# Sixteen graphs through four graph layers on one core: half weighings first in the filling, and one attention's row of powers made by way of DRAM

## The chip, the cores and the metric

The kernel runs on one core of one Trainium2 chip. The metric is the device time of one execution in microseconds (us), the median of several runs; less is better.

## The reference, cut to what matters

There are 16 graphs of N = 1024 nodes with 128 features and a 0/1 adjacency. Four layers follow one another, each `x = x + layer(relu(layernorm(x)), adj)`. The first is a convolution with batch norms over all graphs. Layers 1 and 3 are additive attentions, layer 2 a product attention:

```
e = leaky_relu(s[:, None] + t[None, :], 0.2)         # s, t = Wh @ a_src, Wh @ a_dst
attn = softmax(where(adj > 0, e, -big)); out = attn @ Wh      # layer 3: elu(out)
```

The kernel calls layer 1 A, layer 2 B and layer 3 C. Since exp of a leaky relu of a sum is the larger of two products, A and C need, after factors are taken out, only `weights = max(row, least[j]) * mask`: `row` holds 1024 powers exp(0.8 us) of the scores, the same on all 128 partitions (`row_e`), and `least` one value for each of the 8 partition tiles j. `us` (128 x 8) has the same scores, one to a partition and tile.

## The kernel before, in words

The first layer takes two stages (up to about 440 us of the profile); the third, on which the change bears, holds the other three. Its rounds i = -1 to 18 (`run(i)` on each engine) form a pipeline over graphs: round i weighs A of graph i, then B of graph i - 1, then C of graph i - 2. Rounds 0, 1 and 2 are the **filling**: round 0 has A alone, round 1 A and B, and from round 2 on all three run. There is no planner: for each engine the order is written out by hand in its `run(i)` (DVE L1084, ACT L1401, PE L1650) and in the loops of SP (L823) and POOL (L864), and semaphores join the queues.

- **PE.** `weigh(x, b, c)` (L1584) makes output tile c of 8: eight matmuls over j into a slot of PSUM, two tiles to a slot; `take` waits until the slot's last user is through. The profile has two records for each fp32 matmul, so a tile is 16 records and a weighing of 8 tiles 128. `weigh_half` (L1602) makes tiles 0 to 3 with j outermost, so that each weights tile j serves four output tiles as soon as it is made; before, only the last C uses it. `gram` (L1562) makes B's scores. `turn_h` (L1528), `turn_q` (L1521) and `turn_rows` (L1574) transpose. `values` (L1550) makes Wh, `highest` (L1545) the top of the scores, and `rows` (L1535) spreads one half of `us` over a row by four transposes.
- **PE's order in a round:** `turn_h` of C, the eight `gram` steps with C's `values`, `highest` and first `rows` between them (L1661 to L1670), A's eight tiles with `turn_q`, C's second `rows` and `turn_rows` between them, B's eight tiles with the next A's `turn_h`, `values`, `highest` and `rows`, then C's eight tiles.
- **DVE.** `weights(x, b, j)` (L938) makes one tile of weights. `exponents` (L915) makes `us` and `te`. `shares` (L964) takes the reciprocals of the sums of a finished pair of tiles, `add` (L972) the residual, then come `stats`, `moments` and `shifts` of the next norm. `leaky` and `lower` work on B, `split_g` and `split_ag` make the low halves for `gram`.
- **ACT.** `row_power` (L1299) makes one half of `row_e` from PSUM, `exps` (L1290) makes `least`, `scaled` (L1327) divides a pair of tiles, which frees their slot, `factors` (L1307) makes A's weighed values, `keep_scores` and `score_exps` follow `gram`, `normed` applies a norm, `high_scores` feeds the splits.
- **POOL.** `upper` (L853) masks B's upper rows, eight steps, each after the turned rows of its k; A's `rstd` stands after the second of them.
- **SP.** Loads in a fixed order: A's mask ring (four tiles deep, in pairs), `qT`, C's ring, B's mask, x, and the output.

## Time and profile before

| | |
|---|---|
| median of 3 runs | 1531.18 us (1531.07 to 1531.24) |
| the profiled execution | 1534.19 us |
| its span in the profile | 1532.4 us |
| PE busy | 1402.3 us (92% of the span) |
| DVE busy | 1133.6 us (74%) |
| ACT busy | 826.6 us (54%) |
| POOL busy | 380.9 us (25%) |
| mean granted TensorE clock | 0.963 |

Busy time is summed over the instructions of an engine, and the share is that of the whole span, so an engine with a high share can still stand idle in one stage. A row of a timeline gives the start, the length, the engine, the line of the code, the operation with the tile that it writes and those that it reads, the number of merged instructions and, in brackets, how long the engine had been idle and who ended that. A matmul's end is modelled, so that a row of PE can end some 0.2 us after the next begins: lengths are better taken from start to start. "q" behind an engine marks its queue, that is the issue of a DMA.

### The profile page before, as it was taken

What the parts mean: (1) busy time and instruction counts of PE and PEld (TensorE: products, weight loads), DVE (VectorE), ACT (ScalarE), POOL (GpSimd) and SP (SyncE); (2) the same over time, 40 slices, a digit from 0 to 9 for tenths busy, and PEclk for the clock granted to TensorE, in tenths of its full rate; (3) what the DMA queues carried; (4) which work ended last, traced back from release to release, by engine and by line L of the source; (5) the groups of instructions that cost most, each with busy time, mean ns of one, the idle gap of its engine ahead of it and who ended that gap; (6) DMA issues with size and microseconds to landing.
All of it is one profiled execution on the core that took longest, in us unless ns stands there. A gap on an engine that the chain in (4) does not pass through costs nothing.

```text
span 1532.4 us, 33041 instructions
## 1 busy us (share of the span) xinstructions
PE 1402.3 (92%) x12740; PEld 1269.2 (83%) x12740; DVE 1133.6 (74%) x3270; ACT 826.6 (54%) x1825; POOL 380.9 (25%) x337
## 2 busy tenths in 40 slices
PE   5899999799946679999999999999999999999886
PEld 5899999555536469999999998989999999999786
DVE  4566665687834667888888888888888888887565
ACT  4687778022232455746656566556574665655521
POOL 6334340000010214133132231331313313232120
PEclk9899999799968789999999999999999999999998
DMA  9999992376741122231431313313223143131111
GB/s 206 225 199 206 211 212 69 103 252 233 247 152 45 52 77 76 56 90 38 109 90 50 97 47 93 104 36 104 72 74 90 36 110 90 36 83 22 49 42 43
DMA packets 109599, 161.95 MB, mean 106 GB/s; under 512 B 9472, under 2 KB 61312, under 8 KB 107392
## 3 DMA queue, kind: packets, MB, share of 16 engines
q1 hardware_dynamic: 85248, 117.86, 26.7%
q0 software_dynamic: 19584, 33.56, 11.9%
q10 hardware_dynamic: 4608, 8.39, 1.6%
q8 instruction: 102, 1.67, 0.4%
q14 instruction: 57, 0.47, 0.1%
HBM read 151.40 MB, written 41.94 MB: 126 GB/s over the span
## 4 chain that ended last, share of the span: by engine, by line
PE 44%; DVE 13%; ACT 6%; DVEq 3%; POOL 2%; issue 2%; DMA 0%; ACTq 0%
PE ps L1598 27%; PE ps L1557 4%; DVE wts_A L946 3%; PE ps L1580 3%; PE ps L1532 2%; PE ps L1569 2%; POOL rs_C L851 2%; DVE wts_C L946 2%; PE ps L1571 2%; PE ps L1570 2%; ACT hN L1279 1%; ACT hV L1276 1%; PE ps L1541 1%; DVEq L979 1%; DVE st_C L884 1%
## 5 line engine op out<-in xcount | busy, mean ns | idle before, releaser
L1598 PE MATMUL ps<-hP_A,wts_A 128*128 128x129 f32 x2112 | 255.3, 276 | 3.7 <-DVE wts_A L946 3.0
L862 POOL TENSOR_TENSOR wts_B<-wts_B,off 128x1024 f32<-128x1024 f32 (+7 forms) x128 | 174.5, 1388 | 335.8 <-PE ps L1580 335.8
L1598 PE MATMUL ps<-hV,wts_B 128*128 128x129 f32 x2048 | 246.5, 276 | 4.4 <-DVE wts_B L961 2.6
L1598 PEld LDWEIGHTS ps<-hP_A,wts_A 128*128 128x128 f32 x2112 | 245.3, 192 | 5.0 <-DVE wts_A L946 4.0
L1598 PEld LDWEIGHTS ps<-hV,wts_B 128*128 128x128 f32 x2048 | 238.8, 193 | 5.3 <-issue 3.0
L1598 PE MATMUL ps<-hP_C,wts_C 128*128 128x129 f32 x1920 | 220.1, 274 | 0.0
L1598 PEld LDWEIGHTS ps<-hP_C,wts_C 128*128 128x128 f32 x1920 | 217.4, 191 | 0.5
L946 DVE SCALAR_TENSOR_TENSOR wts_A<-row_A,least_A,ring_A 128x1024 f32<-128x1024 f32 x128 | 160.8, 1274 | 7.5 <-ACT row_A L1304 4.7
L294 ACT ACTIVATE maskT<-ps 128x1024 fp8e4<-128x1024 bf16 x128 | 131.2, 1025 | 59.5 <-PE ps L336 48.2
L946 DVE SCALAR_TENSOR_TENSOR wts_C<-row_C,least_C,ring_C 128x1024 f32<-128x1024 f32 x120 | 160.2, 1346 | 0.0
L348 PE MATMUL ps<-x,adj_b 128*128 128x129 f16 x896 | 122.4, 225 | 16.1 <-ACT whn L277 13.1
L1338 ACT ACTIVATE xB<-ps,rec_A 128x128 f32<-128x128 f32 x128 | 40.1, 364 | 165.1 <-DVE rec_A L970 165.1
L349 PE MATMUL ps<-x,adj_b 128*128 128x128 f16 x896 | 122.7, 224 | 0.0
L952 DVE SCALAR_TENSOR_TENSOR wts_B<-wts_B 128x1024 f32<-128x1024 f32 (+7 forms) x128 | 90.7, 750 | 34.5 <-ACT wts_B L1320 34.5
L348 PEld LDWEIGHTS ps<-x,adj_b 128*128 128x128 bf16 x896 | 89.3, 100 | 19.5 <-ACT whn L277 15.8
L683 PE MATMUL ps<-maskT,row_hi 128*128 128x512 fp8e4 x256 | 97.2, 380 | 0.0
L683 PE MATMUL ps<-maskT,row_lo 128*128 128x512 fp8e4 x256 | 97.0, 379 | 0.0
L851 POOL TENSOR_TENSOR rs_C<-rs_C,mhalf 128x8 f32<-128x8 f32 x16 | 38.7, 2422 | 233.0 <-DVE rs_C L891 233.0
L336 PE MATMUL ps<-ident_bf,adj_b 128*128 128x128 bf16 x1024 | 80.0, 222 | 14.0 <-DMA adj_b<-in_adj 13.1
L1325 ACT ACTIVATE wts_B<-wts_B,shiftB 128x1024 f32<-128x1024 f32 (+7 forms) x128 | 90.3, 772 | 4.3 <-DVE wts_B L952 4.3
L1320 ACT COPY wts_B<-ps 128x1024 f32<-128x1024 f32 (+7 forms) x128 | 78.1, 638 | 26.3 <-PE ps L1571 24.7
L349 PEld LDWEIGHTS ps<-x,adj_b 128*128 128x128 bf16 x896 | 89.5, 100 | 0.0
(234 smaller groups left out, 2694.7 us busy)
## 6 DMA issues: line engine op xcount, KB each, us to landing
adj_b<-in_adj POOLq DMA_DIRECT2D x120, 256.0 KB, 9.8
maskT_scratch<-maskT SPq DMA_DIRECT2D x16, 1024.0 KB, 6.9
ring_A<-maskT_scratch SPq DMA_DIRECT2D x64, 256.0 KB, 3.1
off<-maskT_scratch SPq DMA_DIRECT2D x32, 512.0 KB, 6.4
ring_C<-maskT_scratch SPq DMA_DIRECT2D x64, 256.0 KB, 3.3
xa<-in_x SPq DMA_DIRECT2D x16, 512.0 KB, 4.5
whT_scratch<-whT_s ACTq DMA_DIRECT2D x32, 256.0 KB, 6.5
whT_b<-whT_scratch SPq DMA_DIRECT2D x16, 512.0 KB, 4.8
```

The lines of the kernel that those rows point to most:

```text
L294: nc.scalar.activation(edges[:, b, c, :], psT[c % 2], ACT.Square, scale=EDGE_VALUE ** 0.5, saturate=False, accum_out=sq_all[:, n:n + 1]).t ...
L336: last = nc.tensor.transpose(psT[c % 2][:, r * P:r * P + P], adj_b[:, b % AB, r, c * P:c * P + P], ident_bf[:, :])
L348: nc.tensor.matmul(q[:, 0:GW], adj_rc, h1, start=(r == 0), stop=False)
L349: nc.tensor.matmul(q[:, 0:P], adj_rc, h2, start=False, stop=False)
L683: last = nc.tensor.matmul(psP[par][:, c * HALF:(c + 1) * HALF], part[:, par, t, :], edges[:, b, t, c * HALF:(c + 1) * HALF], start=(t == 0 ...
L851: pool.tensor_tensor(rs_c[x][:, :], rs_c[x][:, :], mhalf[:, :], ALU.pow).then_inc(S[x, "rstd"], 1)
L862: pool.tensor_tensor(w, w, off_fp8[:, k, k * P:N], ALU.mult).then_inc(S["B", "up"], 1)
L946: nc.vector.scalar_tensor_tensor(wts[y][:, j, :], row_e[y][:, :], least[y][:, j:j + 1], ring[x][:, j % MR, :], ALU.max, ALU.mult).then_inc ...
L952: nc.vector.scalar_tensor_tensor(w, w, SLOPE, w, ALU.mult, ALU.max).then_inc(S["B", "lrelu"], 1)
L1320: nc.scalar.copy(wts["B"][:, j, j * P:N], P_SLOTS[j % 2][:, j * P:N]).then_inc(S["B", "kept"], 1)
L1325: nc.scalar.activation(w, w, ACT.Exp, bias=shiftB[:, 0:1]).then_inc(S["B", "exps"], 1)
L1598: last = nc.tensor.matmul(Q_SLOTS[c // 2 % 2][:, c % 2, 0:PW], wts[y][:, j, c * P:c * P + P], src[:, j, :], start=(j == 0), stop=(j == T - 1))
```

## The change

It has two parts.

**Filling.** In rounds 0, 1 and 2 the first four tiles of A are made by `weigh_half`. In round 0 it stands where tile 0 stood, and the next A's `values`, `highest` and `rows` come behind it, before tile 4 and after tiles 4 to 6. In rounds 1 and 2 it stands first in the round, before `gram`; in round 2 C's `turn_h` moves behind the first `gram`. So that the weights are there, DVE makes all of A(1) at the end of round 0 and all of A(2) in round 1: four of A(2)'s tiles now stand before `shares("B", 0, 2)` and four more after `shares("B", 0, 3)`, ahead of the residual and the statistics for C. The first two `shares` and `scaled` of A move to the front of rounds 0 to 2.

**C's row.** For the graphs 0 to 13 of C, `rows` and `row_power` go. In their place ACT takes the power of the 128 x 8 values of `us` and stores them to a scratch row of 1024 values in DRAM with an access pattern that turns them, 4 bytes at a time (`store_row`, after `keep_scores` 7), and SP, in front of its load of `qT`, waits for that store and reads the row to all 128 partitions (`load_row`, 512 KB into SBUF). DVE's first weights of C wait for this load. Graphs 14 and 15 of C, and all of A, keep the old way. The masks, the sums and the results are the same.

The diff, without blank lines, and with 8 of the leading spaces cut:

```diff
@@ -106,2 +106,3 @@
 pTf_dram = nc.dram_tensor("pTf_scratch", (B, P, N), fp32).ap()
+row_dram = {x: nc.dram_tensor(f"row_scratch_{x}", (2, T, P), fp32).ap() for x in "AC"}
 NT = B * T
@@ -720,2 +721,6 @@
     row_e = {x: sbc(f"row_{x}", [P, N]) for x in cases}
+    us_e = {x: a_rep[:, 0, k * T:(k + 1) * T] for k, x in enumerate(cases)}
+    VIA = {"A": range(0), "C": range(0, B - 2)}
     ring = {"A": ring_A, "C": sbc("ring_C", [P, MR, N], u8)}
@@ -760,2 +765,5 @@
     S["C", "quo_exp"] = csem("C_quo_exp")
+    for x in cases:
+        for n in ("s_kept", "s_out", "s_in"):
+            S[x, n] = csem(f"{x}_{n}")
     for n in ("var", "rstd", "shift", "h", "hT_made", "ahi", "lo", "gram", "kept", "lrelu", "exps", "turned", "low", "up", "tile", "rec", "quo", "done"):
@@ -785,2 +793,3 @@
     LT = T - 1
+    EARLY = (1, 2)
     GROUPS_T = ((0, 1), (1, 2), (2, 3), (3, 5), (5, 7))
@@ -788,2 +797,6 @@
+    def turned_rows(x, b):
+        return b - sum(k < b for k in VIA[x])
     def turned(k):
@@ -808,2 +821,11 @@
+            def load_row(x, b):
+                n = b - VIA[x].start
+                sp.wait_ge(S[x, "s_out"], (n + 1) * 16)
+                if b > 0:
+                    sp.wait_ge(S[x, "wts"], b * T)
+                sp.dma_start(row_e[x][:, :], row_dram[x][n % 2].rearrange("t p -> (t p)").partition_broadcast(P)) \
+                    .then_inc(S[x, "s_in"], 16)
             def load_q(b):
@@ -826,2 +848,4 @@
                     load_mask("A", i + 1, 1)
+                if i - 2 in VIA["C"]:
+                    load_row("C", i - 2)
                 if 1 <= i + 2 < B:
@@ -943,3 +967,6 @@
                     dve.wait_ge(S[x, "exp"], b + 1)
-                    dve.wait_ge(S[x, "s_row"], 2 * b + 2)
+                    if b in VIA[x]:
+                        dve.wait_ge(S[x, "s_in"], (b - VIA[x].start + 1) * 16)
+                    else:
+                        dve.wait_ge(S[x, "s_row"], 2 * turned_rows(x, b) + 2)
                 y = home(x, b)
@@ -1096,4 +1123,7 @@
                     shares("C", i - 3, 3)
-                if AA:
+                if AA and i not in EARLY:
                     weights("A", i, 7)
+                if i == 0 or i in EARLY:
+                    shares("A", i, 0)
+                    shares("A", i, 1)
                 if GW:
@@ -1138,3 +1168,3 @@
                     stats("A", newA, 0)
-                if AA:
+                if AA and i > 2:
                     shares("A", i, 0)
@@ -1145,3 +1175,3 @@
                     moments("A")
-                if AA:
+                if AA and i > 2:
                     shares("A", i, 1)
@@ -1203,4 +1233,11 @@
                     weights("C", i - 2, 5)
+                if i == 1:
+                    weights("A", 2, 0)
+                    lowest("A", 2)
+                    weights("A", 2, 1)
                 if GW:
                     add("B", i - 1, 0, newC, oldC)
+                if i == 1:
+                    weights("A", 2, 2)
+                    weights("A", 2, 3)
                 if CA:
@@ -1211,3 +1248,3 @@
                     weights("C", i - 2, 7)
-                if nextA:
+                if nextA and i != 1:
                     weights("A", i + 1, 0)
@@ -1221,3 +1258,9 @@
                     elu_negative(i - 3)
-                if nextA:
+                if i == 0:
+                    for j in range(2, T):
+                        weights("A", 1, j)
+                if i == 1:
+                    for j in range(4, T):
+                        weights("A", 2, j)
+                if nextA and i + 1 not in EARLY:
                     weights("A", i + 1, 2)
@@ -1236,3 +1279,3 @@
                     moments("C")
-                if nextA:
+                if nextA and i + 1 not in EARLY:
                     weights("A", i + 1, 3)
@@ -1245,3 +1288,3 @@
                     split_ag(i)
-                if nextA:
+                if nextA and i + 1 not in EARLY:
                     weights("A", i + 1, 4)
@@ -1252,3 +1295,3 @@
                     shares("C", i - 2, 2)
-                if nextA:
+                if nextA and i + 1 not in EARLY:
                     weights("A", i + 1, 5)
@@ -1299,3 +1342,3 @@
             def row_power(x, b, h):
-                act.wait_ge(S[x, "s_made"], 2 * b + h + 1)
+                act.wait_ge(S[x, "s_made"], 2 * turned_rows(x, b) + h + 1)
                 y = home(x, b)
@@ -1306,2 +1349,14 @@
+            def store_row(x, b):
+                n = b - VIA[x].start
+                act.wait_ge(S[x, "us"], b + 1)
+                if n > 0:
+                    act.wait_ge(S[x, "s_out"], n * 16)
+                nc.scalar.activation(us_e[x], us[x][:, :], ACT.Exp, scale=1.0 - SLOPE).then_inc(S[x, "s_kept"], 1)
+                act.wait_ge(S[x, "s_kept"], n + 1)
+                if n > 1:
+                    act.wait_ge(S[x, "s_in"], (n - 1) * 16)
+                act.dma_start(row_dram[x][n % 2].rearrange("t p -> p t"), us_e[x], allow_slow_non_contiguous=True) \
+                    .then_inc(S[x, "s_out"], 16)
             def factors(x, b, h):
@@ -1413,2 +1468,6 @@
                     scaled("C", i - 3, 3)
+                if i == 2:
+                    scaled("A", i, 0)
+                    scaled("A", i, 1)
+                    keep_scores(i - 1, 0)
                 if CA:
@@ -1416,3 +1475,7 @@
                 if GW:
-                    keep_scores(i - 1, 0)
+                    if i != 2:
+                        keep_scores(i - 1, 0)
+                    if i == 1:
+                        scaled("A", i, 0)
+                        scaled("A", i, 1)
                     keep_scores(i - 1, 1)
@@ -1428,4 +1491,4 @@
                     keep_scores(i - 1, 7)
-                if CA:
-                    row_power("C", i - 2, 0)
+                if CA and i - 2 in VIA["C"]:
+                    store_row("C", i - 2)
                 if GW:
@@ -1433,4 +1496,2 @@
                         score_exps(i - 1, j)
-                if CA:
-                    row_power("C", i - 2, 1)
                 if GW:
@@ -1443,4 +1504,6 @@
                 if AA:
-                    scaled("A", i, 0)
-                    scaled("A", i, 1)
+                    if i not in EARLY:
+                        scaled("A", i, 0)
+                        scaled("A", i, 1)
+                    scaled("A", i, 2)
                     if i == 0:
@@ -1448,3 +1511,2 @@
                         row_power("A", 1, 1)
-                    scaled("A", i, 2)
                 if nextA and i != 0:
@@ -1536,3 +1598,3 @@
-                take(free, 1, S[x, "s_row"], 2 * b + h + 1)
+                take(free, 1, S[x, "s_row"], 2 * turned_rows(x, b) + h + 1)
                 if h == 0:
@@ -1658,3 +1720,5 @@
                 AA, GW, CA, nextA = 0 <= i < B, 1 <= i <= B, 2 <= i <= B + 1, i + 1 < B
-                if CA:
+                if i in EARLY:
+                    weigh_half("A", i)
+                if CA and i != 2:
                     turn_h("C", i - 2, hN, free_q, 0, "hT")
@@ -1664,2 +1728,4 @@
                     if CA:
+                        if i == 2 and j == 0:
+                            turn_h("C", i - 2, hN, free_q, 0, "hT")
                         if j == 1:
@@ -1668,4 +1734,2 @@
                             highest("C", i - 2, free_q, 1)
-                        if j == 4:
-                            rows("C", i - 2, free_q, 0)
                 if i == -1:
@@ -1676,3 +1740,6 @@
                     turn_h("A", 1, hN, free_p, 1, "hT")
-                for c in range(T):
+                    weigh_half("A", 0)
+                    values("A", 1, free_p, 0, T)
+                c0 = T // 2 if 0 <= i <= 2 else 0
+                for c in range(c0, T):
                     if AA:
@@ -1680,14 +1747,12 @@
                     if i == 0:
-                        if c == 0:
-                            values("A", 1, free_p, 0, T)
-                        if c == 1:
+                        if c == 4:
                             highest("A", 1, free_p, 1)
-                        if c in (2, 3):
-                            rows("A", 1, free_p, c - 2)
-                    if c == 0 and nextA and i > 0:
+                        if c in (5, 6):
+                            rows("A", 1, free_p, c - 5)
+                    if c == c0 and nextA and i > 0:
                         turn_q(i + 1)
-                    if c == 0 and CA and AA:
-                        rows("C", i - 2, free_q, 1)
-                    if GW and c < len(GROUPS_T):
-                        turn_rows(i - 1, *GROUPS_T[c])
+                    if GW and c - c0 < len(GROUPS_T):
+                        turn_rows(i - 1, *GROUPS_T[c - c0])
+                if i in EARLY:
+                    turn_rows(i - 1, *GROUPS_T[4])
                 for c in range(T):
```

## Rows read from the trace of the kernel before

**Rows 1.** Ten rounds: length; busy PE, PEld, DVE, ACT, POOL; clock; DMA share; GB/s.

```profile
800.00:1400.00 600.00, 594.13 (x5092) 558.46 (x5091) 510.23 (x1311) 364.63 (x836) 166.47 (x103) 1.00 0.27 73
```

**Rows 2.** PE in order of time, steady state, round i = 3 (start, length).

```profile
642.25 0.60 PE L1541 MATMUL ps<-ident,us_C 128*128 128x128 f32 x4
...
642.87 0.34 PE L1569 MATMUL ps<-g_hi,ag_hi 128*128 128x384 f16 x1
...
647.00 0.60 PE L1541 MATMUL ps<-ident,us_C 128*128 128x128 f32 x4
```

**Rows 3.** ACT in order of time, the same round.

```profile
642.15 1.16 ACT L1320 COPY wts_B<-ps 128x640 f32<-128x640 f32 x2
...
644.64 0.60 ACT L1304 ACTIVATE row_C<-ps 128x512 f32<-128x512 f32 x1
```

**Rows 4.** DVE in order of time, the same round.

```profile
656.00 1.86 DVE L946 SCALAR_TENSOR_TENSOR wts_C<-row_C,least_C,ring_C 128x1024 f32<-128x1024 f32 x1
...
659.63 0.16 DVE L968 TENSOR_SCALAR rec_A<-ps 128x2 f32<-128x2 f32 x1 [0.71 <-PE ps L1598]
...
673.22 0.29 DVE L918 TENSOR_REDUCE top<-ps 128x1 f32<-128x128 f32 x1 [0.48 <-PE ps L1548]
```

**Rows 5.** View of the DMAs: issues, KB each, median us to landing.

```profile
whT_scratch<-whT_s ACTq DMA_DIRECT2D x32, 256.0 KB, 6.5
...
qT<-pTf_scratch SPq DMA_DIRECT2D x16, 512.0 KB, 3.3
```

**Rows 6.** Instructions of line 159, a load in 1024 pieces.

```profile
DMA to landing us min/median/max: 4.2/4.2/4.2
```

**Rows 7.** PE in order of time, rounds i = 0 and 1 of the filling.

```profile
467.56 1.76 PE L1598 MATMUL ps<-hP_A,wts_A 128*128 128x129 f32 x8
...
486.84 7.31 PE L1598 MATMUL ps<-hP_A,wts_A 128*128 128x129 f32 x64
...
506.09 1.97 PE L1532 MATMUL ps<-ident,hV 128*128 128x128 f32 x8 [11.94 <-ACT hP_A L1312]
...
512.72 0.59 PE L1569 MATMUL ps<-g_hi,ag_hi 128*128 128x512 f16 x1 [4.66 <-DVE ag_lo L990]
...
522.47 2.00 PE L1598 MATMUL ps<-hP_A,wts_A 128*128 128x129 f32 x16
...
540.75 3.74 PE L1598 MATMUL ps<-hV,wts_B 128*128 128x129 f32 x32
```

**Rows 8.** DVE in order of time, rounds i = 0 and 1.

```profile
469.40 4.87 DVE L946 SCALAR_TENSOR_TENSOR wts_A<-row_A,least_A,ring_A 128x1024 f32<-128x1024 f32 x4 [0.62 <-DMA ring_A<-maskT_scratch]
...
502.57 1.28 DVE L946 SCALAR_TENSOR_TENSOR wts_A<-row_A,least_A,ring_A 128x1024 f32<-128x1024 f32 x1 [1.98 <-ACT least_A L1297]
...
556.72 1.29 DVE L946 SCALAR_TENSOR_TENSOR wts_A<-row_A,least_A,ring_A 128x1024 f32<-128x1024 f32 x1 [1.43 <-ACT row_A L1304]
```

**Rows 9.** POOL in order of time, rounds i = 1 and 2.

```profile
526.26 2.01 POOL L862 TENSOR_TENSOR wts_B<-wts_B,off 128x1024 f32<-128x1024 f32 x1 [25.88 <-PE ps L1580]
...
533.22 6.14 POOL L862 TENSOR_TENSOR wts_B<-wts_B,off 128x768 f32<-128x768 f32 x6
...
593.27 8.17 POOL L862 TENSOR_TENSOR wts_B<-wts_B,off 128x768 f32<-128x768 f32 x6
```

**Rows 10.** PE in order of time, round i = 2.

```profile
561.33 1.97 PE L1532 MATMUL ps<-ident,hV 128*128 128x128 f32 x8 [2.47 <-ACT hP_A L1312]
...
570.58 1.94 PE L1532 MATMUL ps<-ident,hN 128*128 128x128 f32 x8 [7.28 <-ACT hN L1279]
...
575.83 1.95 PE L1557 MATMUL ps<-w_use,hT_c 128*128 128x130 f32 x16
...
582.33 2.00 PE L1598 MATMUL ps<-hP_A,wts_A 128*128 128x129 f32 x16
...
601.05 3.74 PE L1598 MATMUL ps<-hV,wts_B 128*128 128x129 f32 x32
```

**Rows 11.** PE in order of time, the last round but one.

```profile
1466.38 15.98 PE L1598 MATMUL ps<-hV,wts_B 128*128 128x129 f32 x116 [2.65 <-DVE wts_B L961]
```

## The prediction, made before the change was run

> **What bounds the kernel now.** I read the time by stretches first, then each engine's timeline over the filling (465 to 635 us) and over one steady round, then the DMAs. In the ten steady rounds PE is busy 594.1 of 600 us at full clock, DVE 510.2, ACT 364.6, POOL 166.5 [rows 1]: there only PE work that is taken away, or a wait that appears, moves the time. The filling is another matter: PE stands idle 11.94 us before the first transpose of round 0's B norm and 7.28 us before C's in round 2 [rows 7, 10], and it restarts at half speed each time: 8 transposes last 1.97 us after a rest, 8 weighing records 1.76 us where 64 last 7.31 us later [rows 7], that is 0.22 us a record at the 1.2 GHz level and (with the 0.16 us by which a modelled end runs over taken off) 0.112 us at 2.4 GHz.
>
> **Steady rounds, what goes.** Eight transposes of PE for each of 14 graphs, at 0.11 us some 0.45 us for each half. The two halves are not worth the same. The first stands between gram(4) and gram(5): it starts at 642.25 and would end near 642.70, but gram(5) starts at 642.87 [rows 2], when ACT has copied the third score tile out of its PSUM slot (the first, 640 wide, of a pair that lasts from 642.15 to 643.31 [rows 3], so done near 642.8). That copy does not come earlier, for it stands behind the small exponentials of C. So the first half hides in a wait and is worth 0; its upper bound is the whole 0.45. The second half, at 647.00 [rows 2], has no wait behind it: turned rows and A's tiles follow at once. It is worth 0.45 us, times 13 rounds (3 to 15): **-5.9 us**; that of round 2 is in the sum of the filling. Two ACT powers from PSUM go as well (0.60 us each [rows 3]), but ACT is no bound.
>
> **Steady rounds, what comes.** ACT gets an exponential of 8 columns, a wait for its own result and the issue of a store, together about 0.6 us by estimate, less than the two powers that go. The remaining exponentials come behind it on ACT; POOL and the turned rows read those microseconds later. The row's way is then: store from about 645.2 (where the old power stood, 644.64 [rows 3], plus 0.6), landing, SP's load, landing. The load is 512 KB like qT's, 3.3 us [rows 5], plus 0.3 for its issue. The store has 1024 pieces of 4 bytes; no row has such. From below: qT's 3.3 with 128 pieces. Nearer by count: a load in 1024 pieces of 512 bytes landed after 4.2 us [rows 6]. From above: ACT's own stores, 6.5 us in the busy first stage [rows 5]; nothing excludes still more. I take 4.2, since DMA is only 27% used here [rows 1]: row on all partitions at 645.2 + 4.2 + 3.6 = 653.0. DVE wants it at 656.00 [rows 4], 0.45 earlier in the new frame. Covered by 2.5 us. If that cover goes, DVE stands at `weights("C", b, 0)` with lower(3), lower(4) and A's third `shares` behind it; its next wait (0.71 us at 659.63 [rows 4]) absorbs that much, and no more: from there DVE runs without a gap to 673.2 [rows 4], where PE's top of the next A waits for it, so the rest reaches PE whole. On SP, `load_row` holds up qT's load by some 2 us and, behind it, C's ring; qT is read only after A's last pair (seven tiles of 1.79 after 647.00, that is 659 at the earliest), C's ring waits for DVE's weights anyway. Both cost 0.
>
> The Trainium skill speaks against this store: "DMA: Bandwidth & Descriptors", section "Rules for kernel authors", says that a strided last dimension becomes one descriptor per element and should be rearranged, and that a transpose by access pattern is slower by a factor of 19. The same page's fixed cost of about 2 us for a small DMA would put the landing below my 4.2. No row here shows 4-byte pieces; my sum goes by the rows.
>
> **Round 0.** PE goes from A(0)'s first tile at 467.56 to its last at 486.84 + 7.15 = 494.0 [rows 7], because tile 0 follows DVE (weights tile 7 is made at 469.40 + 4.87 = 474.3 [rows 8]) and because the next A's second `rows` waits for ACT. With four tiles made together PE has 128 + 16 records of A and values, 16.1 us, and 9 transposes, 1.0 us, and I add 1.1 us for records still at the low level (the transposes before lost 1.0 of the same restart). That is 18.2 us, end at 485.8. DVE does not gate it: the half ends at 467.56 + 7.2 + 1.1 = 475.8, after 474.3. All that follows (residual, norm, `turn_h` of B at 506.09) hangs on this end: **-8.2 us**.
>
> **Round 1**, in the old times. From `turn_h` at 506.09: 1.8 for itself, 8.3 for the half (32 products at full rate and 1.1 at the low level), 516.2. DVE's eight weights and two splits end there too: 502.57 [rows 8] + 8 x 1.22 + about 1 for the ring and small steps + 2.4 for the splits (an estimate, two full tiles) = 515.7. gram took 9.75 us from 512.72 to 522.47 [rows 7] and starts warm now: 8.5, to 524.7. From gram's end to POOL's first step 3.8, POOL to its end 13.1 (526.26 to 533.22 + 6.14 [rows 9]), the last product 0.25: 541.9. Before, B's first tile ended at 540.75 + 1.79 = 542.5 [rows 7]. So the half moved away from A comes back as a wait for POOL: only **-0.7 us**. PE works in crumbs for 5 us there; the clock may fall. Bounds of that loss: 0, and 3.0 (116 records took 15.98 us after a 2.65 us rest [rows 11], 13.0 at full rate). I take **+1.1**.
>
> **Round 2**, in old times. The hole of round 1's end is filled by the half of A(2), but DVE now puts four weights before B's third `shares` and four more before C's statistics. From 556.72 [rows 8]: 4 x 1.22 and the residual, 562.4. Behind it on ACT two `scaled` and two `factors`, about 3.8: PE's `turn_h` of B at 566.2 instead of 561.33 [rows 10]. Then 2.0 and 8.2 for the half: 576.4. DVE's path (four more weights 4.9, then residual, statistics, POOL's power and two splits, by estimate 8.5) ends at about 576 too. gram(0) 1.3, then ACT has two `scaled`, one copy and the ReLU ahead of `values`: 580.3. From `values` to gram's end 6.5 as before (575.83 to 582.33 [rows 10]): 586.8, 4.5 late. From gram's end to POOL's end 593.27 + 8.17 - 582.33 = 19.1 [rows 9, 10], less 0.45 for the second `rows`, plus 0.25: 605.7 against 601.05 + 1.79 = 602.8. **+2.9 us**, and for 6 us of crumbs before it the clock's loss once, **+2.2** (bounds 0 and 3.0).
>
> **Sum.** -5.9 - 8.2 - 0.7 + 1.1 + 2.9 + 2.2 = -8.6 us. Span 1532.4, execution 1534.19, so the span's 1532.4 becomes 1523.8; the median of the runs, 1531.18, lies 3.0 below the profiled execution, and the difference carries over: 1522.5.
>
> **The rivals.**
> 1. The first `rows` counts too. For it: gram(5) misses it by only 0.2 us. Against: the copy above. 14 x 0.45 = 6.3 more: 1516. If the clock holds in the filling as well, 1513.
> 2. The filling gains nothing: the late `shares`, POOL and the colder clock eat round 0's gain. For it: two of my three rounds are about zero or worse. Against: round 0 stands by itself. Then only the rows count, 1525.
> 3. The change does not do what it says: PE's time comes back as waits in both places, since DVE runs without a gap into 673.2. Then 5.9 is lost from the sum: 1528.4, no measurable difference.
> 4. The row comes late; slower. Place: `weights("C", b, 0)`. It decides from a store landing of 656.3 - 645.2 - 3.6 = 7.5 us, and the gain is gone at 8.2 (0.6 us x 14 graphs). At 9.5 us, 2 us x 14 = 28: 1550.5. For it: ACT's stores already show 6.5, and 4-byte pieces are in no row. Against: 1024 pieces cost 4.2 in a busier time. A transpose that costs 19 times as much would be this rival; that rule is the Trainium skill's (page and section above), and the trace neither agrees nor disagrees.
>
> **How the numbers follow.** My forecast 0.50, own range 1519 (no clock loss) to 1525; rival 1: 0.18; rival 2: 0.14; rival 3: 0.08; rival 4: 0.10. A measurement of this kernel tells about 0.2% from no change, 3.1 us. Faster by more: forecast and rivals 1 and 2, 0.82; within: rival 3, 0.08; slower: 0.10. The range 1514 to 1528.5 leaves out rival 4 and half of what lies beyond rival 1.
>
> **What would show it.** No us_C records of PE before C's last two graphs; A's last tile of round 0 near 486; gram(5) still 0.6 us after gram(4) ends; a PE wait for POOL at B's first tile in rounds 1 and 2; steady rounds 0.45 us shorter; the first C weights not waiting for a DMA. I am wrong if that wait appears, if rounds shorten by 0.9 or not at all, or if the two waits for POOL are not there.

## The result and the profile after

| | before | changed |
|---|---|---|
| median of 4 runs | 1531.12 us | 1546.38 us (1542.64 to 1548.47) |
| the profiled execution, its span | 1534.19, 1532.4 us | 1545.3, 1543.5 us |
| PE, DVE, ACT, POOL busy | 1402.3, 1133.6, 826.6, 380.9 us | 1398.2, 1118.4, 815.5, 373.8 us |
| mean granted clock of PE | 0.963 | 0.966 |

The ratio of the changed kernel's time to that of the kernel before is 1.0089 (95% interval 1.0074 to 1.0103): 0.9% slower, where I had given faster 0.82 and slower 0.10. It is my rival 4.

The ten steady rounds by stretches, to be held against [rows 1]: PE has lost 12.7 us of busy time in 600 us, and yet the rounds got longer (63.44 us in the mean instead of 62.30, see the table further down).

```profile
800.00:1400.00 600.00, 581.45 (x4924) 540.47 (x4923) 491.48 (x1299) 348.72 (x808) 159.94 (x100) 1.00 0.30 80
```

Where PE's time went stands in the page's chain (shares of the span by engine) and in its costliest groups (busy, mean ns | idle before and who ended it):

```profile
PE 23%; DVE 18%; DMA 12%; ACT 7%; DVEq 5%; issue 4%; POOL 3%; ACTq 0%; SPq 0%
...
L1660 PE MATMUL ps<-hV,wts_B 128*128 128x129 f32 x2048 | 254.9, 281 | 25.9 <-ACT xB L1393 19.8
...
L973 DVE SCALAR_TENSOR_TENSOR wts_C<-row_C,least_C,ring_C 128x1024 f32<-128x1024 f32 x120 | 154.8, 1302 | 50.5 <-DMA row_C<-row_scratch_C 50.5
```

DVE stands 50.5 us in front of C's first weights, over 14 graphs, and waits for the row. PE feels it one step later: B's tiles wait for ACT's `xB`, the `scaled` that frees a slot of PSUM and itself waits for the shares that stand behind those weights on DVE. One steady round in order of time, ACT's power and its store, SP's load, and then DVE and PE (start, length):

```profile
638.35 0.21 ACT L1355 ACTIVATE a_rep<-us_C 128x8 f32<-128x8 f32 x1
638.59 0.37 ACTq L1359 DMA_DIRECT2D row_scratch_C<-a_rep  x1
...
646.97 0.32 SPq L828 DMA_DIRECT2D row_C<-row_scratch_C  x1
...
652.87 1.80 DVE L973 SCALAR_TENSOR_TENSOR wts_C<-row_C,least_C,ring_C 128x1024 f32<-128x1024 f32 x1 [3.52 <-DMA row_C<-row_scratch_C]
...
656.76 3.84 PE L1660 MATMUL ps<-hV,wts_B 128*128 128x129 f32 x32 [0.33 <-ACT xB L1393]
```

SP waits for the store and then issues its load, so the distance of the two issues is the store's price: 8.4 us here, 8.3 to 10.6 over the 14 graphs, median 9.8. (SP has a second wait, for C's weights of the graph before. It does not bind: with another store, in e3 below, the distance is 1.4 us.)

**The filling.** PE in order of time, rounds 0 to 2, for [rows 7, 10]; then POOL for [rows 9]:

```profile
462.21 7.89 PE L1673 MATMUL ps<-hP_A,wts_A 128*128 128x129 f32 x64
...
478.08 1.95 PE L1660 MATMUL ps<-hP_A,wts_A 128*128 128x129 f32 x16
491.96 1.97 PE L1594 MATMUL ps<-ident,hV 128*128 128x128 f32 x8 [11.93 <-ACT hP_A L1367]
...
526.60 4.62 PE L1660 MATMUL ps<-hV,wts_B 128*128 128x129 f32 x22 [0.34 <-POOL wts_B L886]
...
552.87 1.97 PE L1594 MATMUL ps<-ident,hV 128*128 128x128 f32 x8 [7.02 <-ACT hP_A L1367]
...
592.97 5.52 PE L1660 MATMUL ps<-hV,wts_B 128*128 128x129 f32 x32 [7.66 <-ACT xB L1393]
```

```profile
521.39 6.12 POOL L886 TENSOR_TENSOR wts_B<-wts_B,off 128x768 f32<-128x768 f32 x6
...
584.52 6.64 POOL L886 TENSOR_TENSOR wts_B<-wts_B,off 128x768 f32<-128x768 f32 x6
```

In round 2 PE's longest wait, 7.66 us in front of B's tiles, is not for POOL (which ended at 591.16) but for ACT's `xB`, behind DVE's 6.03 us of waiting for the first late row.

**A ruler for what follows.** The third stage does not begin at the same time in each execution: PE's first transposition of hN in it starts anywhere from 446.8 to 452.9 us in the profiles, for kernels that are alike up to there. So I measure the third stage from that record to the span's end, and rounds from one `turn_h` of B to the next. These repeat closely: round 4 lasted 61.75 us before and 61.76 in each of three experiments that left it alone. (The columns: the marker to round 1's `turn_h` of B, which holds round 0; rounds 1 to 3; rounds 4 to 15; the rest; the whole. Us; the labels are those of the experiments below.)

```
kernel                     start   r 1-3   r 4-15   rest    third stage
before                     53.9    180.3   739.3    106.7   1080.2
changed                    45.2    189.6   755.6    106.3   1096.7
e1_fill_only               45.6    188.8   739.3    106.9   1080.6
e2_row_only                54.2    182.5   754.1    106.7   1097.5
e3_flat_store              45.3    188.5   738.1    105.3   1077.2
e4_round0_only             45.4    179.9   739.3    106.8   1071.4
e5_early1                  45.5    179.7   739.5    106.7   1071.4
e6_pe_row                  45.2    180.8   738.3    106.7   1071.0
e7_pe_row_swap             45.5    179.2   734.1    106.6   1065.3
e8_swap_only               46.3    179.7   736.8    106.6   1069.4
e9_pieces8                 47.1    186.6   738.3    105.2   1077.2
e10_store_early            45.4    185.0   740.6    106.7   1077.6
e11_store_early_swap       45.4    179.2   735.6    105.3   1065.6
```

Already the first two lines say it: 8.7 us gained by round 0, 9.3 lost again in rounds 1 to 3, 16.3 lost in twelve steady rounds.

### The profile page after: what moved, and what is told of

Its sections match the earlier page's. It is cut to its first block, busy times and chain, and to the rows that moved or that the text cites. A ratio compares the mean times of both kernels' runs of the same rounds, so it can differ in the third digit from the quotient of the medians.

```text
span 1543.5 us, 32844 instructions
## 1 busy us (share of the span) xinstructions
PE 1398.2 (91%) x12628; PEld 1260.1 (82%) x12628; DVE 1118.4 (72%) x3270; ACT 815.5 (53%) x1811; POOL 373.8 (24%) x337
## 4 chain that ended last, share of the span: by engine, by line
PE 23%; DVE 18%; DMA 12%; ACT 7%; DVEq 5%; issue 4%; POOL 3%; ACTq 0%; SPq 0%
PE ps L1660 11%; DMA row_scratch_C<-a_rep 8%; DMA row_C<-row_scratch_C 4%; DVE wts_C L973 4%; PE ps L1619 4%; DVE wts_A L973 3%; DVEq L996 2%; PE ps L1673 2%; POOL rs_C L875 2%; PE ps L1594 2%; ACT wts_B L1375 1%; ACT hV L1319 1%; PE ps L1631 1%; ACT hN L1322 1%; DVE xC L1050 1%
## 5 line engine op out<-in xcount | busy, mean ns | idle before, releaser
L1660 PE MATMUL ps<-hV,wts_B 128*128 128x129 f32 x2048 | 254.9, 281 | 25.9 <-ACT xB L1393 19.8
L1660 PEld LDWEIGHTS ps<-hV,wts_B 128*128 128x128 f32 x2048 | 243.8, 196 | 32.5 <-ACT xB L1393 24.8
L886 POOL TENSOR_TENSOR wts_B<-wts_B,off 128x1024 f32<-128x1024 f32 (+7 forms) x128 | 168.3, 1341 | 330.8 <-PE ps L1642 330.8
L1660 PE MATMUL ps<-hP_A,wts_A 128*128 128x129 f32 x1920 | 230.2, 275 | 0.7 <-ACT xB L1393 0.7
L1660 PEld LDWEIGHTS ps<-hP_A,wts_A 128*128 128x128 f32 x1920 | 221.6, 191 | 0.9 <-ACT xB L1393 0.9
L973 DVE SCALAR_TENSOR_TENSOR wts_C<-row_C,least_C,ring_C 128x1024 f32<-128x1024 f32 x120 | 154.8, 1302 | 50.5 <-DMA row_C<-row_scratch_C 50.5
L337 PE MATMUL ps<-ident_bf,adj_b 128*128 128x128 bf16 x1024 | 79.8, 222 | 13.3 <-DMA adj_b<-in_adj 13.3
```

The source lines that it names most:

```text
L337: last = nc.tensor.transpose(psT[c % 2][:, r * P:r * P + P], adj_b[:, b % AB, r, c * P:c * P + P], ident_bf[:, :])
L886: pool.tensor_tensor(w, w, off_fp8[:, k, k * P:N], ALU.mult).then_inc(S["B", "up"], 1)
L973: nc.vector.scalar_tensor_tensor(wts[y][:, j, :], row_e[y][:, :], least[y][:, j:j + 1], ring[x][:, j % MR, :], ALU.max, ALU.mult).then_inc ...
L1660: last = nc.tensor.matmul(Q_SLOTS[c // 2 % 2][:, c % 2, 0:PW], wts[y][:, j, c * P:c * P + P], src[:, j, :], start=(j == 0), stop=(j == T - 1))
```

## The experiments

Each ratio below is that to the kernel before, run beside the experiment; its medians there were 1532.4 to 1533.1 us, so medians of different experiments are compared with care, and the stages of the profiles decide. "Third stage" is the last column of the table above.

### Taking the change apart

**e1_fill_only**: the filling of the change, C's row in the old way.

```diff
-    VIA = {"A": range(0), "C": range(0, B - 2)}
+    VIA = {"A": range(0), "C": range(0)}     # and rows, row_power back in their places ...
```

> The filling of the change with C's row made the old way by PE and ACT in every round. Theory R (the store of the row in 4-byte pieces lands after more than 8 us, so that DVE's first weights of C wait, and this costs more than the whole change brings): the filling by itself gains a little, 1 to 3 us, since only round 0 gains (8 to 9 us) and rounds 1 and 2 give most of it back: 1528 to 1530. Rival F (the reordered DVE and ACT work of the filling is what costs): 1540 or more.

Measured: 1530.68 us, ratio 0.9981 (0.9965 to 0.9997); third stage 1080.6, before 1080.2. The filling taken alone is worth 0.2% by the medians, as expected, and nothing in the third stage of the profile; either way it is not what costs.

**e2_row_only**: the filling of before, the row by way of DRAM.

```diff
-    EARLY = (1, 2)
+    EARLY = ()                               # and round 0 by eight single tiles, as before ...
```

> The filling as before, C's row by way of DRAM. Theory R: PE saves some 0.45 us in each of 13 rounds, but DVE waits 3 to 4 us for the row and PE gets about 1.8 us of that: 1.3 to 1.4 us slower for each of 14 rounds, 1548 to 1551. Rival F: the row gains, 1525.

Measured: 1550.54 us, ratio 1.0118 (1.0094 to 1.0143); third stage 17.3 us longer. DVE's longest waits, 600 to 1400 us (total, times, longest):

```profile
DVE wts_C L970 <- DMA row_C<-row_scratch_C: 40.7, 12, 4.2
```

So the whole loss is the row's. Together e1 and e2 make 17.7 us, the change has 16.5. In rounds 1 to 3 the two make 10.7 us and the change 9.3: in its round 2 PE waits for the late row while POOL finishes, instead of for POOL as in e1.

### What is wrong with the row

**e3_flat_store**: the changed kernel, with the same 4 KB stored as 128 pieces of 32 bytes, each partition's eight values side by side (they land in another order, so C weighs with a permuted row).

```diff
-act.dma_start(row_dram[x][n % 2].rearrange("t p -> p t"), us_e[x], allow_slow_non_contiguous=True)
+act.dma_start(row_dram[x][n % 2].rearrange("t p -> (t p)").rearrange("(p t) -> p t", t=T), us_e[x])
```

> As the changed kernel, but the 128 x 8 powers are stored untransposed, 128 pieces of 32 bytes instead of 1024 of 4 bytes; the row then holds its 1024 values in another order (this is left out: the transposition of the row). Everything else, the load to all partitions included, is the same. Theory R: the store lands in 2 to 4 us, DVE's wait for the row goes, and the time falls by 20 us or more, to 1520 to 1526. Rival L (the load from one 4 KB row to 128 partitions, or SP's queue, is what is late): the wait stays near 3 us and the time above 1538.

Measured: 1528.27 us (1527.78 without the one far-off execution named below), ratio 0.9963 (0.9952 to 0.9974), third stage 1077.2. The DMAs (count, KB each, median us to landing):

```profile
row_C<-row_scratch_C SPq DMA_DIRECT2D x14, 512.0 KB, 4.0
...
row_scratch_C<-a_rep ACTq DMA_DIRECT2D x14, 4.0 KB, 1.4
```

DVE's wait is gone, and 19.5 us of the third stage come back by the shape of the store alone; the load, 4.0 us here, is not what was late. The 20 us or more that I expected of the whole time came as 18 to 19. (One of the ten executions took 4240 us and is not in the ratio; it has no trace, and its cause stays open.)

**e9_pieces8**: the changed kernel with 512 pieces of 8 bytes (two values of a partition stay together, so the order is wrong again, differently).

```diff
-act.dma_start(row_dram[x][n % 2].rearrange("t p -> p t"), us_e[x], allow_slow_non_contiguous=True)
+act.dma_start(row_dram[x][n % 2].rearrange("t p -> (t p)").rearrange("(t p k) -> p t k", p=P, k=2),
+              us_e[x].rearrange("p (t k) -> p t k", k=2), allow_slow_non_contiguous=True)
```

> The changed kernel with the row stored in 512 pieces of 8 bytes (left out: two neighbouring values of the row then stand in another order). The store in 1024 pieces of 4 bytes landed after 8.4 us, that in 128 pieces of 32 bytes after 1.4 us. Theory N (the cost goes by the number of pieces, 7.8 ns each over a floor): it lands at 4.4 us, DVE's wait goes almost entirely, and the time is within 2 us of the flat store's. Rival W (pieces under 32 bytes are slow in DRAM whatever their number): 7 us or more, and DVE waits some 2 us a round.

Measured: 1529.22 us, ratio 0.9971 (0.9953 to 0.9989), third stage 1077.2 as in e3. From its DMAs:

```profile
row_scratch_C<-a_rep ACTq DMA_DIRECT2D x14, 4.0 KB, 3.8
```

The price rises with the number of pieces: from issue to issue 1.4 us for 128, 3.9 for 512, 9.8 for 1024. It is no fixed price for each piece: from 128 to 512 pieces one more costs some 6 ns, from 512 to 1024 some 12. The 4 KB are always the same, so more pieces are also smaller pieces, and no run here parts the two; rival W, that anything under 32 bytes takes 7 us or more, is refuted. The page's table of queues counts them (packets, MB, share); before, this queue had 4608 packets, and 14,560 more in 14 stores are 1040 each, 16 above the 1024 values. First the changed kernel, then e9, where it is 528:

```profile
q10 hardware_dynamic: 19168, 8.45, 2.0%
```

```profile
q10 hardware_dynamic: 12000, 8.45, 1.8%
```

The Trainium skill ("DMA: Bandwidth & Descriptors", "Rules for kernel authors") has it that a strided last dimension becomes one descriptor for each element; the packet count agrees. The factor of 19 that the Trainium skill gives there is that of a rearranged pattern against the hardware's own DMA transpose, which no run here has. Against the plain store of e3 the turned one takes 7 times as long (9.8 to 1.4).

**e10_store_early**: the changed kernel with all its 1024 pieces; only the place moves. ACT takes the power right behind C's other exponentials, and SP issues the store.

```diff
 exps("C", i - 2)
+store_row("C", i - 2)                # now the exponential alone
...
 def load_row(x, b):
+    sp.wait_ge(S[x, "s_kept"], n + 1)
+    sp.dma_start(row_dram[x][n % 2].rearrange("t p -> p t"), us_e[x], allow_slow_non_contiguous=True).then_inc(S[x, "s_out"], 16)
     sp.wait_ge(S[x, "s_out"], (n + 1) * 16)
... (the store goes from ACT's queue)
```

> The changed kernel with the same 1024 pieces of 4 bytes, but the power of C's scores is taken right behind C's other exponentials and SP issues the store itself, some 2.5 to 3 us earlier in the round. Theory late (the store costs its 8.4 us of landing and nothing else, and the row is about 3.5 us late at DVE's first weights of C): DVE's wait for the row falls from 3.5 us a round to under 1 us, the mean round from 63.44 to between 62.2 and 62.6 us, the third stage to 1077 to 1083 us. Theory traffic (the small pieces also slow other transfers or engines): the wait falls as well, but the rounds stay above 63 us.

Measured: 1530.21 us, ratio 0.9973 (0.9958 to 0.9987), third stage 1077.6. The store still takes 9.3 us (median of 14, 8.2 to 10.6), and DVE's wait in 600 to 1400 us is down from 40.4 us to

```profile
DVE wts_C L978 <- DMA row_C<-row_scratch_C: 10.8, 13, 1.1
```

The mean round falls from 63.44 to 62.44 us; e3 has 62.23. So the small pieces do little other harm than to come late: started 2.5 us sooner in the round (18.04 us after `turn_h` of B instead of 20.56), the slow store is nearly hidden. The Trainium skill's advice to issue a DMA early and wait late (same page and section) is what the trace shows: with 2.5 us of it the third stage is 19 us shorter, 15.0 of them in rounds 4 to 15, where the shape of the transfer gave 17.5. (The rest is in rounds 1 to 3, and 1.4 us of it is PE's clock, see the account of the prediction below. The edit also takes the issue of the store off ACT, whose next exponentials start 0.55 us sooner; no run parts that from the earlier store.)

### The filling

**e4_round0_only**: half weighing in round 0 alone, old rows.

```diff
-    EARLY = (1, 2)
+    EARLY = ()                               # and C's row as in e1, A's order in rounds 1 and 2 as before ...
```

> Of the change only round 0's half weighing (with the shares, values, highest and rows that it moves); rounds 1 and 2 and C's row as before. Theory: round 0's gain of 8.2 to 8.8 us passes through whole, since everything later hangs on the end of A(0): 1522 to 1523. Rival: the next chain (POOL, DVE) takes it back and less than 4 us is left: 1527 or more.

Measured: 1524.2 us, ratio 0.9937 (0.9913 to 0.996); third stage 8.8 us shorter than before, so round 0's gain passes through whole.

**e5_early1**: rounds 0 and 1, but not 2: DVE makes all of A(1) in round 0 and nothing of A(2) ahead of B's shares. Against e4:

```diff
-    EARLY = ()
+    EARLY = (1,)                             # with A(1)'s weights, shares and scaled as in the change ...
```

> The filling of the change without round 2's part: half weighings in rounds 0 and 1, DVE's order for A(2) as before; C's row made the old way. Round 0 alone took 8.8 us from the third stage; rounds 0, 1 and 2 together took nothing. Theory D (DVE's eight early weights of A(2), ahead of the shares of B and the statistics of C, are what gives the gain back): the third stage is 7 to 9 us shorter than before, since round 1's half weighing by itself is worth about 0. Rival P (each half weighing moved ahead of gram comes back as a wait for POOL and a colder clock): 2 to 5 us shorter only.

Measured: 1522.44 us, ratio 0.9944 (0.9927 to 0.996); third stage 1071.4, the same as e4. The half of round 1 is worth 0: rounds 1 and 2 took 54.8 and 62.9 us against 55.2 and 62.5 in e4. All that e1 lacks against e4, 9.2 us, therefore comes with the half of round 2 and its four early and four later weights in round 1; no run parts the half from the weights. The rows point to two things. B's third shares stand behind four weights on DVE (`turn_h` of B in round 1 to that in round 2: 60.9 us in e1, 54.8 in e5), and PE waits some 7.0 us in front of the second `turn_h`, 2.5 in e5. And in round 2, 65.9 us against 62.9, POOL ends last and is slow: its six steps took 9.20 us, 8.18 in e5. POOL in e1, for [rows 9] and the 6.64 us above:

```profile
587.94 9.20 POOL L886 TENSOR_TENSOR wts_B<-wts_B,off 128x768 f32<-128x768 f32 x6
```

PE in e1 then goes on at the 1.2 GHz level (granted clock 0.50), 18 records in 4.24 us, where they would take some 2.2 at the prediction's 0.112 us a record:

```profile
597.20 4.24 PE L1662 MATMUL ps<-hV,wts_B 128*128 128x129 f32 x18 [0.56 <-POOL wts_B L886]
```

### Why the transpositions that went were worth so little

The rows' 0.9 us a round are gone in e3, and a steady round fell only from 62.31 (e1) to 62.23 us. The first half of `rows` went into a wait: PE's waits for ACT's copies between the gram steps, over the 13 rounds in 600 to 1400 us, are 9.2 us in e3 and 3.2 in e1, 0.46 more a round. The second half is there at first: in one round of e3 PE's turned rows stand 0.44 us earlier in the round, as forecast, but at the top of the next A 0.40 of it is lost, for DVE reaches `peak_A` no sooner, having worked without a wait from 719.99 us to the end of `peak_A` at 733.50.

**e8_swap_only**: e4 with C's fifth weights tile moved on DVE behind the next A's `columns`, so that the peak which PE waits for comes one tile (some 1.2 us) sooner.

```diff
-weights("C", i - 2, 4)
 columns("A", i + 1)
+weights("C", i - 2, 4)
 exponents("A", i + 1)
```

> Round 0's half weighing, C's row the old way, and the same swap on DVE. Theory S: PE waits for DVE only 0.1 us there without the shorter row, so at most 0.1 us a round, 1 us in all; the swap pays only together with the row. Rival: the swap alone brings 4 us or more.

**e6_pe_row**: e4 with C's row by DRAM, but turned by one PE transposition (128x8 to 8x128), so that the store has 8 pieces of 512 bytes.

```diff
+nc.tensor.transpose(LAST[x][0:T, 0:P], us[x][:, :], ident[:, :])
...
-act.dma_start(row_dram[x][n % 2].rearrange("t p -> p t"), us_e[x], allow_slow_non_contiguous=True)
+act.dma_start(row_dram[x][n % 2], a_rep[0:T, 1, 0:P])
```

> Round 0's half weighing, and C's row by way of DRAM with one transposition by PE first: us (128 x 8) is turned to 8 x 128 between two gram steps, ACT takes its power there and stores 8 pieces of 512 bytes. Theory: the store lands in about 1.5 us and no wait for the row appears; but, as with the flat store, a steady round gets only 0.04 to 0.07 us shorter, since PE's 0.44 us comes back as a wait for DVE in front of the next A's top: 0.5 to 1 us better than round 0 alone, 1522 to 1524. Rival: the flat store's gain was held down by its wrong row, and 5 us more come: 1518.

**e7_pe_row_swap**: both.

> As the run before, and on DVE the fifth weights tile of C moves from before the next A's columns to between its columns and its exponents. Theory S (DVE's unbroken work up to that top is what holds PE's saved 0.44 us): the 12 steady rounds get 0.4 us shorter each, 5 us in all: 1517 to 1519. Rival T (the saved time is held elsewhere too, at the norm of C or by POOL): less than 2 us: 1521 or more.

Measured, beside e4:

```
                     us       ratio (95%)               mean of rounds 4-14
e4_round0_only       1524.2   0.9937 (0.9913, 0.996)    62.31
e6_pe_row            1520.32  0.9924 (0.9904, 0.9943)   62.25
e8_swap_only         1518.05  0.992  (0.9893, 0.9948)   62.08
e7_pe_row_swap       1516.83  0.991  (0.9889, 0.993)    61.87
```

Without the swap the new row saves 0.06 us a round, with it 0.21. The swap alone saves 0.23 with the old rows, some 2.5 us over rounds 4 to 15, where I had expected 1 us at most. DVE's waits for PE's `highest` in 600 to 1400 us, first e6, then e7:

```profile
DVE top L942 <- PE ps L1595: 7.2, 13, 1.4
```

```profile
DVE top L942 <- PE ps L1596: 1.7, 9, 0.2
```

So the meeting of DVE and PE at the next A's peak held the round; it is shown by the swap, which changes nothing else. The swap does two things at once, and no run parts them: the peak comes sooner, and DVE works on C's tile where it stood waiting for `highest` (in e4 7.2 us over these rounds, in e8 2.0). The second may be why it pays with the old rows too. The chain of what ended last in e4 leaves PE at `highest` and comes back to it only at C's `turn_h`, by way of DVE, of POOL's `rs_C` for C's norm and of ACT's `hN`:

```profile
848.90 0.31 PE ps L1591
...
849.23 0.29 DVE top L942
...
863.59 2.61 POOL rs_C L875
...
872.56 1.07 PE ps L1575 x8
```

Over 600 to 1400 us PE's weighing (L1641) holds 41.8% of this chain and `rs_C` 2.9%; in e8 it is 60.2% (there L1642) and 1.0%. With the swap in place the new row is worth 0.21 of the 0.45 us a round that its second half was to give. In e7 the weighing (L1646) holds 53.5% of the chain and `rs_C` 1.6%, so that some rounds are held there again; the rest stays open. In e6 the store takes 1.2 us. e7 beats both kernels.

**e11_store_early_swap**: the half in round 0 alone, the early store of e10 with its 1024 pieces, and the swap.

> The half weighing in round 0 alone, the row of powers by the early store of 4-byte pieces as in the run beside this, and C's fifth weights tile behind A's columns as in the best kernel so far. Theory late: rounds of 61.9 to 62.2 us (the eight transpositions gone, less what is left of the wait), third stage 1066 to 1070 us, within 2 us of the kernel whose row is turned by PE (1065.3). Theory traffic: rounds above 62.5 us and a third stage above 1074 us.

Measured: 1517.01 us, ratio 0.9899 (0.9882 to 0.9916), mean round 61.99, third stage 1065.6 against 1065.3 of e7. The slow store, issued in time, does as well as the one turned by PE in the whole. In the steady rounds it is 0.12 us a round behind (DVE still waits 12.8 us for the row over the 14 graphs), and the last rounds make up for it.

## Why the prediction was wrong, step by step

The step that failed is "**Steady rounds, what comes**", and in it the row's landing: the forecast had the row there 2.5 us before DVE wants it, and it came 3.5 us late.

- **When the store starts: right.** 20.8 us after `turn_h` of B forecast (645.2 to 624.4), 20.5 measured (638.59 to 618.0).
- **The store: 4.2 us taken, 9.8 measured (8.3 to 10.6).** I chose by count of pieces the nearest row, 1024 pieces of 512 bytes [rows 6], and kept ACT's 6.5 [rows 5] as the bound from above, though I had written that nothing excludes more. The nearest row by one measure was no neighbour: it was a load, not a store, of far larger pieces, and it took 4.2 us where the store took 9.8, so the count alone is not the price. Rival 4's threshold of 7.5 us lay between my two bounds and what came.
- **The load: 3.3 us taken from qT [rows 5], 4.6 measured.** In this round the row was 5.9 us behind SP's issue, 2.3 more than forecast. 4.2 too little for the store, 2.3 for the load, less 0.3 for the earlier start, is 6.2 us, against 2.5 of cover: 3.7. DVE stood 3.5.
- **"that much, and no more": wrong the other way.** I let DVE's next wait absorb 0.7 us and PE take the rest. Between 600 and 1400 us DVE stood 40.4 us, and the rounds there grew by 15 (13 of 1.14). Two entries of DVE's balance make up the other 25; this is read from the traces and no experiment shows it. DVE's waits for PE in `shares` of A fell from 25.7 us to 13.3. And DVE is busy 51.97 us a round instead of 52.98 (491.48 and 510.23 of 600 us, times the round), another 13: it now stands while POOL works (in the round above POOL's six steps run from 648.88 to 655.55 us and DVE stands until 652.87), and the last section shows what the two cost each other. So rival 4 had the place and the mechanism, and its price for 9.5 us (28 us) was too high.
- **The second half of `rows`, -5.9 us: wrong, a second step that failed.** It came out earlier at PE and was lost at the next A's peak (e3 against e1: 1.3 us over rounds 4 to 15 are left of it). That is rival 3's mechanism, which I gave 0.08; the swap shows it.
- **The first half, 0: right**, and for the reason given: in the changed kernel as in e3 PE's waits for ACT's copies in `gram` are 9.2 us instead of 3.2 in 13 rounds.
- **Round 0, -8.2: right.** From the marker to `turn_h` of B it is 8.7 us shorter, and e4, which has this part alone, is 8.8 us shorter in the third stage.
- **Rounds 1 and 2, +5.5: within the scatter, at its low end, and in part by luck.** They took 118.3 us before and, in the five profiles with this filling, 122.9 (e10) to 126.7 (e1): 4.6 to 8.5 more, 7.8 in the changed kernel. PE's wait for POOL in round 1 is where I put it. That in round 2 is there in e1 and e3 but not in the changed kernel, where the late row stands in its place. In round 1 the times differ by PE's clock: the same 22 records behind the same wait took 4.62 us in the changed kernel, at a granted clock of 0.67, and in e10, at 1.00,

```profile
530.96 3.24 PE L1660 MATMUL ps<-hV,wts_B 128*128 128x129 f32 x22 [0.34 <-POOL wts_B L891]
```

Sum by what was measured in the third stage: -8.7 (start), +9.3 (rounds 1 to 3), +16.3 (4 to 15), -0.4 (rest): +16.5 us. The two profiled executions differ by 11.1 only, since the changed one reached the marker 5.4 us sooner, within what that moment scatters; the medians differ by 15.3.

## What to carry to other kernels

A transfer that replaces work of an engine is judged by when its result is there, so price the store, the load and the two issues from rows of the same kind and the same size of piece, and if there is none, measure it before the rest: one store decided this change. If it is too slow, start it earlier before giving it up; 2.5 us sooner gave back 15.0 of the 16.3 us that it had cost in the steady rounds. And work taken from a busy engine is only worth what the next meeting with the other busy engine lets through: look for that meeting, and move a step that nobody waits for from before it to behind it.

## What the hardware showed that I had not expected

- A store of 4 KB in 4-byte pieces held back the load that waits for it 8.2 to 10.6 us, one in 8-byte pieces 2.9 to 4.4, in 32-byte pieces 1.4, and in 512-byte pieces 1.2 (from issue to issue; single ones of the last two took 2.4 and 3.4).
- POOL and DVE slow each other. POOL's same six steps took 6.64 us where DVE stood waiting for the row, 9.20 in e1 where DVE was at work. In round 1 of the changed kernel it was DVE alone that paid: POOL took 6.12 us, and DVE's residual `xB` in that stretch 1.82 us instead of 0.67 in round 2 after POOL had ended. DVE in e1 over that stretch, and in the changed kernel after POOL had ended, shows the same small step and the same two weights:

```profile
590.09 1.28 DVE L920 SCALAR_TENSOR_TENSOR sf_A<-mv_A,rs_A 128x8 f32<-128x8 f32 x1
...
591.83 3.46 DVE L973 SCALAR_TENSOR_TENSOR wts_C<-row_C,least_C,ring_C 128x1024 f32<-128x1024 f32 x2
```

```profile
592.77 0.16 DVE L920 SCALAR_TENSOR_TENSOR sf_A<-mv_A,rs_A 128x8 f32<-128x8 f32 x1
...
593.38 2.47 DVE L973 SCALAR_TENSOR_TENSOR wts_C<-row_C,least_C,ring_C 128x1024 f32<-128x1024 f32 x2
```

The Trainium skill ("SBUF — State Buffer", "Who interferes with whom") says that these two engines share a pair of ports which one holds at a time while the other stands. The rows agree in kind: DVE's step of 0.16 us lasts 1.28 and ends at 591.37 us, when a step of POOL ends (1.80 us from 589.55).
- Steady rounds that a kernel leaves alone repeat to 0.04 us, while the stages before them move by up to 6 us. Without the ruler of rounds, differences of 0.1 us a round could not have been read.
